# Feed-forward part written out by group, with norms, transposes, beta and gamma beside its matmuls, and x loaded in two pieces

## The chip, the cores and the metric

The kernel runs on one core of a Trainium2 chip, in float32. The metric is the device time of one execution in microseconds (us); of several runs the median counts. The core has five engines with instruction streams of their own: TensorE (PE in the profile, its weight loads PEld), VectorE (DVE), ScalarE (ACT), GpSimd (POOL) and SyncE (SP, which here only issues DMAs). They meet through semaphores alone.

## What is computed

One layer: `xn = norm(x)`, and the output is `x + attention(xn) + ffn(xn)`, where attention normalizes a second time and returns its own residual too.

```python
x = L0_attn_x                                  # (16, 256, 128): 4096 rows of 128
xn = _layernorm(x, axis=-1)
# attention (16 heads of 64, a recurrence over 256 steps), on xn:
xn2 = (xn - mu) / jnp.sqrt(var + LN_EPS) * ln_w + ln_b
beta = jax.nn.sigmoid(xn2 @ Wb.T + bb)         # gamma alike
# ... q, k, v, decays, two states S and R, output projection, + xn
# FFN, on xn:
h = jax.nn.silu(_tlin(x, w1_w, w1_s)) * _tlin(x, w2_w, w2_s)      # 128 -> 512
h = jax.nn.gelu(_tlin(h, h1_w, h1_s), approximate=False)          # 512 -> 512
h = jax.nn.gelu(_tlin(h, h2_w, h2_s), approximate=False)          # 512 -> 512
return _tlin(h, w3_w, w3_s)                                       # 512 -> 128
```

## The kernel before

The 4096 rows lie in 32 tiles of 128 rows, side by side in one SBUF tile `xa` of 128x4096. The program has four stages, one behind the other, and the order in each is written by hand, engine by engine.

**Prologue.** SP issues all loads on one queue: x whole (L239), the constants with the identity (L240), small vectors, then the FFN's weights, all of which count on one semaphore `ld_ffn` (L247 to L254). VectorE and ScalarE normalize all 32 tiles at once, twice: sum and mean (L729, L730), centred rows (L731), squares on ScalarE (L1111), their sum (L735, L736), the root on ScalarE (L1113), reciprocal and product (L738, L739). L741 starts `acc`, to which everything is added. TensorE transposes the 32 tiles of the first norm into the eight PSUM banks and later those of the second norm (L338); ScalarE copies them to `xnT` (L1121) and, with the affine of the second norm, to `xhT` (L1123). TensorE then makes the products of beta and gamma from `xhT` (L345, 128 matmuls with 16 columns), VectorE adds their biases (L746), ScalarE takes the sigmoids (L1129). The weights' wait and that for the biases (`bg_add`) stand ahead of the FFN.

**FFN.** A hardware loop over eight groups of 512 tokens: first layer with its gate (L355, L356, 8 matmuls of 128x512), second (L365, 16), third (L373, 16), last (L379, 16 matmuls with 128 columns). ScalarE does silu (L1136) and gelu (L1139, L1142) between them, VectorE the product with the gate (L754), the last scale and the sum into `acc` (L757, L760). Layers 2, 3 and the last use banks 4 and 5, 6 and 7, and 4.

**Zeroing.** Only behind the last sum (`ffn_added`) VectorE writes ones and zeros into `rst` and the six attention buffers `AS` and `AR` (L764, L766), GpSimd into `lane_id`, `lane_x` and `XF` (L1099). Behind both (`ready`), SP writes the zeros of `XF` to DRAM (L256) and loads the projection weights `wt` (L260); the attention buffers lie where the FFN's were, since the two scopes of SBUF take turns.

**Attention.** 64 quads (4 head groups by 16 batches), software-pipelined by `body(k)` on each engine, written out in full, 32.3 us a quad (2070.2 us by 64). It starts on TensorE with the projections of k and q (L396, L399), which need `wt`.

## Time and profile before

| what | us |
|---|---|
| median of 3 runs (range) | 2472.81 (2470.99 to 2474.99) |
| the profiled execution, its own time | 2473.48 |
| its span | 2471.7 |
| prologue, until the first FFN matmul | 76.6 |
| FFN | 309.3 |
| from there to the first attention matmul | 15.6 |
| attention | 2070.2 |

The span runs from the first to the last instruction that the profile shows; 1.8 us of the execution lie outside it. The four stages are cuts at moments that the trace shows, and add up to the span.

### The profile page before, as it was taken

What the parts mean: (1) busy time and instruction counts of PE and PEld (TensorE: products, weight loads), DVE (VectorE), ACT (ScalarE), POOL (GpSimd) and SP (SyncE); (2) the same over time, 40 slices, a digit from 0 to 9 for tenths busy, and PEclk for the clock granted to TensorE, in tenths of its full rate; (3) what the DMA queues carried; (4) which work ended last, traced back from release to release, by engine and by line L of the source; (5) the groups of instructions that cost most, each with busy time, mean ns of one, the idle gap of its engine ahead of it and who ended that gap; (6) DMA issues with size and microseconds to landing.
All of it is one profiled execution on the core that took longest, in us unless ns stands there. A gap on an engine that the chain in (4) does not pass through costs nothing.

```text
span 2471.7 us, 119622 instructions
## 1 busy us (share of the span) xinstructions
PE 2299.7 (93%) x52544; PEld 1928.8 (78%) x52544; DVE 1754.5 (71%) x3725; ACT 1055.5 (43%) x1616; POOL 1286.6 (52%) x2440
## 2 busy tenths in 40 slices
PE   1999995799999999999999999999999999999997
PEld 1544543588888888888888888888888888888886
DVE  6101013688888878888888788888888888888884
ACT  2323222444444444444444444444444444444430
POOL 0000002656666656666666566666666666666661
PEclk8899997699999999999999999999999999999999
DMA  2000000111111121211111212111112122222221
GB/s 87 1 0 0 0 0 20 27 39 37 37 37 37 37 47 37 39 37 37 37 37 37 43 37 40 37 38 37 37 36 48 38 39 41 41 41 41 41 41 27
DMA packets 306089, 84.77 MB, mean 34 GB/s; under 512 B 280368, under 2 KB 302512, under 8 KB 305584
## 3 DMA queue, kind: packets, MB, share of 16 engines
q1 hardware_dynamic: 305584, 77.25, 15.6%
q8 instruction: 414, 6.78, 1.2%
q14 instruction: 91, 0.75, 0.1%
HBM read 41.53 MB, written 35.65 MB: 31 GB/s over the span
## 4 chain that ended last, share of the span: by engine, by line
PE 59%; issue 20%; DVE 14%; ACT 3%; DMA 2%; SPq 1%; POOL 1%; DVEq 0%; ACTq 0%; POOLq 0%
PE bank L454 10%; PE bank L434 3%; DVE Kt L823 3%; PE bank L416 3%; PE bank L405 3%; PE bank L489 3%; PE bank L498 3%; PE bank L396 3%; PE bank L411 3%; PE bank L613 3%; PE bank L423 2%; PE bank L580 2%; PE bank L399 2%; PE bank L531 2%; PE bank L522 2%
## 5 line engine op out<-in xcount | busy, mean ns | idle before, releaser
L1080 POOL TENSOR_TENSOR lane_t<-lane_n,lane_x 128x15 f32<-128x15 f32 (+7 forms) x960 | 326.7, 340 | 110.2 <-DMA lane_n<-n_dram 34.1
L1083 POOL TENSOR_TENSOR lane_x<-lane_x,lane_t 128x15 f32<-128x15 f32 (+7 forms) x960 | 340.5, 355 | 75.2
L454 PE MATMUL bank<-kq,Kt 64*64 64x96 f32 x8192 | 367.0, 233 | 7.1 <-issue 5.6
L454 PEld LDWEIGHTS bank<-kq,Kt 64*64 64x64 f32 x8192 | 315.2, 134 | 59.3 <-issue 58.9
L1032 POOL TENSOR_TENSOR dk<-cum 128x512 f32<-128x512 f32 x64 | 68.8, 1075 | 297.4 <-DVE cum L800 297.4
L1047 POOL TENSOR_TENSOR KQF<-efull,kn 128x768 f32<-128x768 f32 x64 | 119.5, 1867 | 161.1 <-ACT efull L1196 161.1
L1099 POOL MEMSET lane_id<- 128x256 f32 x1 | 0.3, 312 | 387.1 <-DVE acc L760 387.1
L757 DVE TENSOR_TENSOR dn<-bank,s3b 128x512 f32<-128x512 f32 x8 | 5.5, 692 | 239.5 <-PE bank L379 239.5
L1156 ACT ACTIVATE q<-bank 128x512 f32<-128x512 f32 x64 | 38.2, 597 | 317.3 <-PE bank L399 269.1
L1230 ACT ACTIVATE oS<-bank 128x512 f32<-128x512 f32 x64 | 38.2, 597 | 302.9 <-PE bank L602 302.9
L1165 ACT ACTIVATE ea<-bank,nba 128x256 f32<-128x256 f32 x256 | 107.5, 471 | 124.7 <-PE bank L405 103.3
L800 DVE TENSOR_TENSOR_SCAN cum<-rst,dk 128x512 f32<-128x512 f32 x128 | 157.5, 1231 | 3.3 <-ACT dk L1177 3.3
L777 DVE TENSOR_SCALAR ea<-ea 128x512 f32<-128x512 f32 x64 | 27.7, 433 | 180.3 <-ACT ea L1165 180.3
L851 DVE COPY_PREDICATED AS<-cst,bank 128x384 f32<-128x384 int32 x256 | 142.8, 584 | 16.5 <-PE bank L454 16.2
L823 DVE TENSOR_TENSOR Kt<-ek,kn 128x512 f32<-128x512 f32 x128 | 135.6, 1100 | 0.0
L542 PE MATMUL bank<-AS,yS 64*64 64x64 f32 x2048 | 133.2, 223 | 0.9 <-ACT oS L1230 0.6
L477 PE MATMUL bank<-Zf,dk 64*64 64x32 f32 x4096 | 131.5, 219 | 1.9 <-issue 1.1
L1051 POOL TENSOR_TENSOR KQF<-ea,KQF 128x384 f32<-128x384 f32 x64 | 77.6, 1213 | 103.4 <-ACT ea L1171 103.4
L554 PE MATMUL bank<-yS,AS 64*64 64x64 f32 x2048 | 129.6, 220 | 1.3 <-DVE Sst L883 1.0
L477 PEld LDWEIGHTS bank<-Zf,dk 64*64 64x64 f32 x4096 | 127.3, 136 | 2.6 <-issue 1.6
L598 PE MATMUL bank<-AR,yR 64*64 64x64 f32 x2048 | 128.4, 218 | 0.0
L1048 POOL TENSOR_TENSOR KQF<-efull,q 128x768 f32<-128x768 f32 x64 | 118.5, 1851 | 0.0
(156 smaller groups left out, 6632.4 us busy)
## 6 DMA issues: line engine op xcount, KB each, us to landing
XF<-x_dram SPq DMA_DIRECT2D x256, 64.0 KB, 2.3
lane_n<-n_dram SPq DMA_DIRECT2D x128, 124.0 KB, 2.8
x_dram<-lane_x SPq DMA_DIRECT2D x128, 124.0 KB, 2.3
n_dram<-AS SPq DMA_DIRECT2D x256, 32.0 KB, 2.0
n_dram<-AR SPq DMA_DIRECT2D x256, 32.0 KB, 1.7
wt<-in_win SPq DMA_DIRECT2D x4, 640.0 KB, 4.6
out_y<-acc SPq DMA_DIRECT2D x16, 128.0 KB, 3.0
hw<-in_h1T SPq DMA_DIRECT2D x1, 1024.0 KB, 5.9
```

What stands on the lines that cost most here:

```text
L454: ins = pe.matmul(v3(dst[hd[h], o:o + kinds * C], kinds)[:, :, i * SUB:(i + 1) * SUB], Kt[hd[h], m * 96 + i * SUB:m * 96 + i * SUB + C], r ...
L477: ins = pe.matmul(IV[hd[h], m * SUB:(m + 1) * SUB], P0[hd[h], m * C:(m + 1) * C], v4(Zf[n % 2][hd[h], :], NM, 2)[:, m, :, BASE:], start=Tr ...
L542: pe.matmul(o, pc(yS[c % 2], p)[hd[h], :], prod(n, 0, c, p, 1)[hd[h], :], start=(c == 0 and p == 0), stop=False, skip_group_check=True)
L554: ins = pe.matmul(o, prod(n, 0, c, p, 2)[hd[h], :], pc(yS[c % 2], p)[hd[h], :], start=True, stop=(c == 0), skip_group_check=True)
L598: ins = pe.matmul(o, pc(yR[c % 2], p)[hd[h], :], prod(n, 1, c, p, 1)[hd[h], :], start=False, stop=(c == 0), skip_group_check=True)
L800: dve.tensor_tensor_scan(cum[:, o], rst[:, :], dk[:, o], 0.0, ALU.mult, ALU.add).then_inc(s["cum"], 1)
L823: ins = dve.tensor_tensor(v4(Kt[:, y * 8 * 96:(y + 1) * 8 * 96], 8, 3)[:, :, 0:3:2, :], v4(ek[:, y * 2 * T:(y + 1) * 2 * T], 8, 2), v4(kn[ ...
L851: dve.copy_predicated(v3(dst, reps), mask, v3(src[:, 0:reps * kinds * C], reps)).then_inc(s["pr_sb"], 1)
L1047: pool.tensor_tensor(kv[:, KF_S:KF_R + 1:3], ef, late(kn), ALU.mult).then_inc(s["kf"], 1)
L1048: pool.tensor_tensor(kv[:, QF_S:QF_R + 1:3], ef, late(q), ALU.mult)
L1080: pool.tensor_tensor(tv, lane_n[:, m * SUB + m + 1:m * SUB + BASE].unsqueeze(2).to_broadcast([L, rows, m + 1]), xv[:, m, 0:m + 1].unsqueez ...
L1083: pool.tensor_tensor(xv[:, m + 1:, 0:m + 1], xv[:, m + 1:, 0:m + 1], tv, ALU.subtract).then_inc(s["lane_step"], 1)
```

## The change

The FFN is no longer a loop: its eight groups are written out, with functions `first_layer(g)` to `last_layer(g)`. Between them stand pieces of the former prologue.

- **Loads.** SP issues only the first 4 tiles of x, then `w1` and its scales, then each layer's weights with a semaphore of their own. ScalarE's queue issues the constants, `w2` and the other 28 tiles of x.
- **Norms.** `norm(i, ...)` runs three times on VectorE alone but for the root (the squares are now a VectorE product): tiles 0 to 3 ahead of the FFN; tiles 4 to 31 behind group 0's `hidden`; the second norm, all 32 tiles, behind group 1's. ScalarE's roots for the last two stand between two gelus of the third layer.
- **Transposes** go four at a time through bank 7, in 16 turns: the first ahead of the FFN, then one in group 0, three in each of groups 1 to 4, two in group 5. Beta's and gamma's products follow in two halves, in group 5 ahead of the last layer and in group 6 behind the first; their biases on VectorE are both in group 6, the sigmoids on ScalarE in groups 6 and 7.
- **Banks.** Layers 2 and 3 share banks 4 and 5, the last layer has bank 6.
- **Zeroing** is GpSimd's alone, behind turns 8 and 16. For that `AS`, `AR`, `rst`, `XF`, `lane_x`, `lane_id`, `wt`, `wo` and `ea` have SBUF of their own, at other addresses than before, and SP's zeros and load of `wt` wait only for GpSimd.
- Attention waits for the last sum into `acc`, as before.

TensorE, ahead of the FFN and in its first matmuls: before (`bank<-cst` are transposes, `bank<-wbg` beta's and gamma's products, `w`, `hw` the FFN's weights):

```order
L338 MATMUL bank<-cst,xc 128x128 x32
L338 MATMUL bank<-cst,sq 128x128 x32
L345 MATMUL bank<-wbg,xhT 64x16 x128
L351 UNCONDITIONAL_BRANCH
L351 ISA
L355 MATMUL bank<-xnT,w 128x512
```

and now, from the start to the last layer of group 0:

```order
L349 MATMUL bank<-cst,xc 128x128 x4
L379 MATMUL bank<-xnT,w 128x512
L380 MATMUL bank<-xnT,w 128x512
...
L393 MATMUL bank<-hA,hw 128x512 x16
L406 MATMUL bank<-hB,hw 128x512 x16
L349 MATMUL bank<-cst,xc 128x128 x4
L418 MATMUL bank<-w,hA 128x128 x16
```

and in groups 5 (its end) and 6:

```order
L406 MATMUL bank<-hB,hw 128x512 x16
L367 MATMUL bank<-wbg,xhT 64x16 x64
L418 MATMUL bank<-w,hA 128x128 x16
L379 MATMUL bank<-xnT,w 128x512
...
L380 MATMUL bank<-xnT,w 128x512
L367 MATMUL bank<-wbg,xhT 64x16 x64
L393 MATMUL bank<-hA,hw 128x512 x16
```

Of 320 instructions' worth of transposes and small products, only four transposes still stand ahead of the FFN; the rest stands between its layers.

VectorE in group 0, now (`hA` is the product with the gate, `dn` the scaled last layer; the first row stands behind the norm of the first 4 tiles):

```order
L803 SCALAR_TENSOR_TENSOR hA<-bank,sc,silu 128x512 x4
L787 TENSOR_REDUCE st<-xa 128x28
L788 TENSOR_SCALAR st<-st 128x28
L789 TENSOR_TENSOR xc<-xa,st 128x3584
L790 TENSOR_TENSOR sq<-xc 128x3584
L791 TENSOR_REDUCE st<-sq 128x28
L792 TENSOR_SCALAR st<-st 128x28
L794 RECIPROCAL st<-st 128x28
L795 TENSOR_TENSOR xc<-xc,st 128x3584
L833 TENSOR_TENSOR acc<-xa,xc 128x4096
L815 TENSOR_TENSOR dn<-bank,s3b 128x512
```

Before, the first and the last of these rows followed each other with nothing between; a norm of 28 tiles and the start of `acc` now lie there.

ScalarE in group 0, now (`hB` is layer 2's gelu, `hA` layer 3's):

```order
L1193 DMA xa<-in_x 128x28x128
L1195 ACT_TABLE_LOAD
L1195 ACTIVATE small<-small 128x1
L1199 ACTIVATE st<-st,small 128x4
L1203 ACTIVATE xnT<-bank 128x512
...
L1227 ACTIVATE hB<-bank,sc 128x512 x4
L1227 ACTIVATE hA<-bank,sc 128x512
L1199 ACT_TABLE_LOAD
L1199 ACTIVATE st<-st,small 128x28
L1227 ACT_TABLE_LOAD
L1227 ACTIVATE hA<-bank,sc 128x512 x3
```

The root of the 28 tiles, with a table load on either side, has moved between the first and the second gelu of layer 3. The diff, cut to its core:

```diff
+        AS = ring("AS", 3, NCH * 2 * 3 * C)
+        AR = ring("AR", 3, NCH * 2 * 2 * C)
+        rst = sb("rst", 2 * T)
+        XF = sb("XF", NM * C)
+        lane_x = sb("lane_x", LANE_W)
+        lane_id = sb("lane_id", BASE * BASE)
+        wt = sb("wt", WCOLS)
+        wo = sb("wo", 2 * DM)
+        ea = sb("ea", 4 * T)
...
         @block.sync
         def _(sp):
-            sp.dma_start(xa[:, :].rearrange("p (n m) -> p n m", n=NBLK), x.rearrange("(n p) m -> p n m", p=P)).then_inc(s["ld_x"], 16)
-            sp.dma_start(cst[:, :], consts).then_inc(s["ld_const"], 16)
+            def tiles(t, lo, hi):
+                return t[:, lo * DM:hi * DM].rearrange("p (n m) -> p n m", n=hi - lo), x[lo * P:hi * P, :].rearrange("(n p) m -> p n m", p=P)
+
+            sp.dma_start(*tiles(xa, 0, 4)).then_inc(s["ld_x0"], 16)
+            sp.dma_start(w1[:, :], w1T).then_inc(s["ld_up"], 16)
+            sp.dma_start(sc[:, 0:4], s1).then_inc(s["ld_up"], 16)
+            sp.dma_start(sc[:, 4:8], s2).then_inc(s["ld_up"], 16)
+            sp.dma_start(v3(hw1[:, :], 4), h1T.rearrange("(k p) n -> p k n", p=P)).then_inc(s["ld_h1"], 16)
+            sp.dma_start(sc[:, 8:12], sh1).then_inc(s["ld_h1"], 16)
+            sp.dma_start(v3(hw2[:, :], 4), h2T.rearrange("(k p) n -> p k n", p=P)).then_inc(s["ld_h2"], 16)
+            sp.dma_start(sc[:, 12:16], sh2).then_inc(s["ld_h2"], 16)
+            sp.dma_start(v3(w3[:, :], 4), w3T.rearrange("(k p) n -> p k n", p=P)).then_inc(s["ld_w3"], 16)
+            sp.dma_start(s3b[:, :], s3.partition_broadcast(P)).then_inc(s["ld_w3"], 16)
             sp.dma_start(lnp[:, 0:1], lnw).then_inc(s["ld_small"], 16)
             sp.dma_start(lnp[:, 1:2], lnb).then_inc(s["ld_small"], 16)
             sp.dma_start(wbg[:, :], wbg_in).then_inc(s["ld_small"], 16)
...
-            sp.dma_start(w1[:, :], w1T).then_inc(s["ld_ffn"], 16)
-            sp.dma_start(w2[:, :], w2T).then_inc(s["ld_ffn"], 16)
-            sp.dma_start(v3(hw1[:, :], 4), h1T.rearrange("(k p) n -> p k n", p=P)).then_inc(s["ld_ffn"], 16)
-            sp.dma_start(v3(hw2[:, :], 4), h2T.rearrange("(k p) n -> p k n", p=P)).then_inc(s["ld_ffn"], 16)
-            sp.dma_start(v3(w3[:, :], 4), w3T.rearrange("(k p) n -> p k n", p=P)).then_inc(s["ld_ffn"], 16)
-            for i, w in enumerate((s1, s2, sh1, sh2)):
-                sp.dma_start(sc[:, 4 * i:4 * i + 4], w).then_inc(s["ld_ffn"], 16)
-            sp.dma_start(s3b[:, :], s3.partition_broadcast(P)).then_inc(s["ld_ffn"], 16)
-            sp.wait_ge(s["ready"], 2)
+            sp.wait_ge(s["ready"], 1)
...
-            pe.wait_ge(s["bg_add"], 2)
-            with pe.Fori(0, GROUPS) as gi:
+            def turn(i, src, gr):
+                if i:
+                    pe.wait_ge(s["xnT_sb"], i)
...
+            def first_layer(g):
+                if g == 0:
+                    pe.wait_ge(s["ld_up"], 16 * 4)
+                pe.wait_ge(s["xnT_sb"], g + 1)
                 for o in range(4):
+                    n = 4 * g + o
+                    if n >= 2:
+                        pe.wait_ge(s["h1_sb"], n - 1)
+                    tok = xnT[:, g * FFN_TOK:(g + 1) * FFN_TOK]
...
+            def second_layer(g):
+                if g == 0:
+                    pe.wait_ge(s["ld_h1"], 16 * 2)
+                for o in range(4):
+                    if o < 2 and g:
+                        pe.wait_ge(s["g2_sb"], 4 * g - 2 + o + 1)
...
+            def third_layer(g):
+                if g == 0:
+                    pe.wait_ge(s["ld_h2"], 16 * 2)
                 for o in range(4):
+                    pe.wait_ge(s["g1_sb"], 4 * g + 3 + (o > 0))
...
+            def last_layer(g):
+                if g == 0:
+                    pe.wait_ge(s["ld_w3"], 16 * 2)
+                else:
+                    pe.wait_ge(s["down_used"], g)
                 for tb in range(4):
...
+            turn_xn(0)
+            for g in range(GROUPS):
+                first_layer(g)
+                if 1 <= g <= 2:
+                    turn_xn(3 * g - 1)
+                elif 3 <= g <= 5:
+                    turn_xh(3 * g - 9)
+                elif g == 6:
+                    beta_gamma(1)
+                second_layer(g)
+                if 1 <= g <= 2:
+                    turn_xn(3 * g)
+                elif 3 <= g <= 5:
+                    turn_xh(3 * g - 8)
+                third_layer(g)
+                if g <= 2:
+                    turn_xn(3 * g + 1)
+                elif 3 <= g <= 4:
+                    turn_xh(3 * g - 7)
+                elif g == 5:
+                    beta_gamma(0)
+                last_layer(g)
+
+            pe.wait_ge(s["ffn_added"], GROUPS)
+            pe.wait_ge(s["bg_add"], 2)
...
-                dve.tensor_tensor(n3(cen), n3(src), bc(mean), ALU.subtract).then_inc(s["x_ready"], 1)
-                dve.wait_ge(s["x_ready"], i + 1)
...
+                link(dve.tensor_tensor(n3(tmp), n3(cen), n3(cen), ALU.mult))
                 link(dve.tensor_reduce(var, n3(tmp), axis=AX.X, op=ALU.add))
                 dve.tensor_scalar(var, var, 1.0 / DM, None, ALU.mult).then_inc(s["stat_ready"], 1)
...
-                dve.wait_ge(s["xn_ready"] if i == 0 else s["norm_done"], 1)
-            dve.tensor_tensor(acc[:, :], xa[:, :], xc[:, :], ALU.add).then_inc(s["acc_init"], 1)
...
-                dve.tensor_tensor(v3(bsum[:, n * 512:(n + 1) * 512], 32), v3(bank[n][:, :], 32),
-                                  bbg[:, :].unsqueeze(1).to_broadcast([P, 32, 4 * QD]), ALU.add).then_inc(s["bg_add"], 1)
-            dve.wait_ge(s["acc_init"], 1)
-            dve.wait_ge(s["ld_ffn"], 16 * 10)
-            dve.drain().then_inc(s["ffn_added"], 1)
                 for o in range(4):
-                    dve.wait_ge(s["silu_sb"], gi * 4 + o + 1)
+                    n = 4 * g + o
+                    dve.wait_ge(s["silu_sb"], n + 1)
+                    if g:
+                        dve.wait_ge(s["down_ps"], g)
...
+            norm(0, xa, xc, sq, xc, 0, 4)
+            dve.wait_ge(s["ld_up"], 16 * 4)
+            for g in range(GROUPS):
+                hidden(g)
+                if g == 0:
+                    dve.wait_ge(s["ld_x"], 16)
+                    norm(1, xa, xc, sq, xc, 4, NBLK)
+                    dve.wait_ge(s["xn_ready"], 2)
+                    dve.tensor_tensor(acc[:, :], xa[:, :], xc[:, :], ALU.add).then_inc(s["acc_init"], 1)
+                elif g == 1:
+                    dve.wait_ge(s["acc_init"], 1)
+                    norm(2, xc, sq, xa, sq, 0, NBLK)
+                    dve.wait_ge(s["ld_small"], 16 * 6)
+                    dve.tensor_scalar(nba[:, :], nba[:, :], -1.0, None, ALU.mult).then_inc(s["nba"], 1)
+                elif g == 6:
+                    add_bias(0)
+                    add_bias(1)
+                add_ffn(g)
+
-            dve.memset(rst[:, :], 1.0)
-            for t in AS + AR:
-                dve.memset(t[:, :], 0.0)
-            dve.drain().then_inc(s["zeroed"], 1)
-            dve.wait_ge(s["zeroed"], 2)
-            dve.memset(rst[:, 0:2 * T:C], 0.0)
-            dve.drain().then_inc(s["ready"], 1)
-            dve.wait_ge(s["ready"], 2)
+            dve.wait_ge(s["ready"], 1)
...
-            pool.wait_ge(s["ffn_added"], GROUPS + 1)
-            pool.wait_ge(s["bg_ready"], 1)
+            pool.wait_ge(s["xn_ready"], 3)
+            pool.wait_ge(s["xnT_ps"], 8)
+            for t in AS + AR:
+                pool.memset(t[:, :], 0.0)
+            pool.memset(rst[:, :], 1.0)
+            pool.wait_ge(s["xnT_ps"], 16)
...
-            pool.wait_ge(s["ready"], 2)
+            pool.wait_ge(s["ready"], 1)
+            pool.wait_ge(s["ffn_added"], GROUPS)
+            pool.wait_ge(s["bg_ready"], 1)
...
+            act.dma_start(cst[:, :], consts).then_inc(s["ld_const"], 16)
+            act.dma_start(w2[:, :], w2T).then_inc(s["ld_up"], 16)
+            act.dma_start(xa[:, 4 * DM:].rearrange("p (n m) -> p n m", n=NBLK - 4), x[4 * P:, :].rearrange("(n p) m -> p n m", p=P)).then_inc(s["ld_x"], 16)
+            act.wait_ge(s["consts_set"], 1)
+            act.activation(small[:, 3:4], small[:, 2:3], ACT.Sqrt, bias=small[:, 2:3]).then_inc(s["root_set"], 1)
...
+                    if g < 2 and layer == 1 and o == g:
+                        roots(g + 1, *((4, NBLK) if g == 0 else (0, NBLK)))
+
+            roots(0, 0, 4)
+            keep_xn(0)
+            act.wait_ge(s["ld_up"], 16 * 4)
...
+                if g == 0:
+                    act.wait_ge(s["ld_h1"], 16 * 2)
+                gelus(g, 0)
+                if 1 <= g <= 2:
+                    keep_xn(3 * g)
+                elif 3 <= g <= 5:
+                    keep_xh(3 * g - 8)
+                elif g >= 6:
+                    squash(g - 6)
+                if g == 0:
+                    act.wait_ge(s["ld_h2"], 16 * 2)
+                gelus(g, 1)
...
+            act.wait_ge(s["ffn_added"], GROUPS)
+            act.wait_ge(s["ready"], 1)
             act.wait_ge(s["nba"], 1)
```

## Rows read from the trace of the kernel before

**Rows 1.** Busy time by stage: length, engines' us (instructions), clock, DMA share, GB/s.

```profile
0.00:33.80 33.80, 0.00 (x0) 0.01 (x1) 18.62 (x11) 6.50 (x4) 0.21 (x4) 1.00 0.52 158
33.80:76.60 42.80, 23.05 (x320) 22.49 (x320) 24.12 (x11) 15.80 (x23) 0.00 (x0) 0.68 0.00 1
76.60:385.90 309.30, 308.38 (x896) 150.25 (x896) 33.72 (x46) 87.62 (x117) 0.00 (x0) 0.99 0.00 0
385.90:401.50 15.60, 0.01 (x1) 0.04 (x1) 8.69 (x10) 0.00 (x0) 1.80 (x4) 0.66 0.21 76
401.50:2471.70 2070.20, 1968.31 (x51328) 1756.04 (x51328) 1669.40 (x3648) 945.56 (x1473) 1284.61 (x2432) 0.98 0.19 38
```

**Rows 2.** Timeline of the prologue: start, us, engine, line, out<-in [idle before].

```profile
11.00 4.42 DVE L729 TENSOR_REDUCE st<-xa 128x32 f32<-128x4096 f32 x1 [10.06 <-DMA xa<-in_x]
28.51 0.32 ACT L1113 ACTIVATE st<-st,small 128x32 f32<-128x32 f32 x1 [3.47 <-DVE st L736]
28.87 0.35 DVE L738 RECIPROCAL st<-st 128x32 f32<-128x32 f32 x1 [0.39 <-ACT st L1113]
74.97 1.29 DVE L746 TENSOR_TENSOR bsum<-bank,bbg 128x512 f32<-128x512 f32 x2 [14.03 <-PE bank L345]
75.70 2.02 ACT L1129 ACTIVATE betas<-bsum 128x128 f32<-128x128 f32 x8 [10.86 <-DVE bsum L746]
```

**Rows 3.** DMA issues (us to landing last) and one microsecond's busy time.

```profile
0.80 0.89 SPq L239 DMA_DIRECT2D xa<-in_x  x1
1.75 5.41 SPq L240 DMA_DIRECT2D cst<-in_consts  x1
w<-in_w1T SPq DMA_DIRECT2D x1, 256.0 KB, 2.9
5.00:6.00 1.00, 0.00 (x0) 0.00 (x0) 0.00 (x0) 0.00 (x0) 0.00 (x0) 1.00 1.05 289
```

**Rows 4.** Busy time in single microseconds of transposes and small products.

```profile
58.00:59.00 1.00, 1.00 (x6) 1.00 (x6) 1.00 (x1) 0.93 (x2) 0.00 (x0) 0.50 0.00 0
60.00:61.00 1.00, 1.00 (x12) 1.00 (x11) 0.94 (x2) 1.00 (x3) 0.00 (x0) 1.00 0.00 0
64.00:65.00 1.00, 1.00 (x41) 1.00 (x40) 0.00 (x0) 0.84 (x1) 0.00 (x0) 1.00 0.08 16
67.00:68.00 1.00, 1.00 (x24) 1.00 (x24) 0.00 (x0) 0.00 (x0) 0.00 (x0) 0.50 0.00 0
```

**Rows 5.** Timeline of the FFN's first group and the start of its second.

```profile
76.61 2.07 PE L355 MATMUL bank<-xnT,w 128*128 x2 [1.69 <-DVE bsum L746]
85.52 13.90 PE L365 MATMUL bank<-hA,hw 128*128 128x512 f32 x32
86.44 0.75 DVE L754 SCALAR_TENSOR_TENSOR hA<-bank,sc,silu 128x512 f32<-128x512 f32 x1 [0.99 <-ACT silu L1136]
99.25 13.90 PE L373 MATMUL bank<-hB,hw 128*128 128x512 f32 x32
102.89 0.69 ACT L1142 ACTIVATE hA<-bank,sc 128x512 f32<-128x512 f32 x1 [2.75 <-PE bank L373]
112.98 4.11 PE L379 MATMUL bank<-w,hA 128*128 128x128 f32 x32
```

**Rows 6.** TensorE's waits in the FFN: us in total, times, longest.

```profile
PEld bank L379 <- ACT hA L1142: 2.4, 8, 0.3
```

**Rows 7.** Timeline from the FFN's end to attention's first gate.

```profile
386.75 0.69 DVE L760 TENSOR_TENSOR acc<-acc,dn 128x512 f32 x1
401.49 2.04 PE L396 MATMUL bank<-xhT,wt 128*128 128x256 f32 x4 [15.62 <-DMA wt<-in_win]
405.10 0.60 ACT L1156 ACTIVATE q<-bank 128x512 f32<-128x512 f32 x1 [22.45 <-PE bank L399]
405.71 1.28 ACT L1165 ACT_TABLE_LOAD   x1
407.01 0.84 ACT L1165 ACTIVATE ea<-bank,nba 128x256 f32<-128x256 f32 x2
```

236 lines of the change are left out of this document (118 added, 118 removed).

## The prediction

> **What bounds the kernel now.** I read the busy times by stage first, since shares of the whole span would mix four stages with different limits. The reader is to see there [rows 1] that TensorE has no matmul in the first 33.8 us, is busy 23.05 us of the next 42.8, and that 76.6 us go by before the FFN begins. In the FFN it is busy 308.38 of 309.3 us and nothing else matters. Then it stands still for 15.6 us, and attention takes 2070.2 us with TensorE busy 1968.31 of them. The change does not touch attention's instructions, so the question is how much of 76.6 and 15.6 us goes, and what the FFN has to pay for taking the prologue's work in.
>
> The second view is the timeline of the prologue [rows 2]. It is one chain: x lands at 11.0 us, and each step on 4096 columns takes 4.42 us on VectorE; after two norms come the transposes, then beta and gamma, and the biases at 74.97. The third is the timeline of an FFN group [rows 5], which gives the slots into which the work moves; the fourth is the end of the FFN [rows 7].
>
> **Removed ahead of the FFN.** Its first matmul runs at 76.61 [rows 5]. I work out the new moment, F.
> - The first 4 tiles of x are 256 KB. A load of 256 KB took 2.9 us from issue to landing [rows 3]. It now shares the engines with the constants of the other queue, and at 289 GB/s [rows 3] another 256 KB are 0.9 us. From an issue at 0.8, x is there between 3.7 and 4.6; I take 4.6.
> - The norm of 512 columns: five big steps. By the 4096-column step one would be 4.42/8 = 0.55 us; the 128x512 step that adds the FFN to `acc` took 0.69 [rows 7]. I take 0.65, so 3.25. Two small steps, root (0.32 [rows 2]), reciprocal and handovers: 0.8. Ready at 8.7.
> - Four transposes at half clock: 6 a us [rows 4], 0.65, with the start 0.9. Copy to SBUF 0.60, as the copy of `q` [rows 7], and a handover. F = 10.3.
>
> By then `w1` and `w2`, issued right behind, are there by the same 2.9 us. The gain is 76.61 - 10.3 = 66.3 us, with bounds of 63 and 68 us: F is 8.5 with the lower ends, 13 if the first landing takes 7 us, between these 2.9 and the whole x's 10.1 (11.0 less the issue at 0.8).
>
> The FFN's first layer took 85.52 - 76.61 = 8.9 us for 8 matmuls, where the 16 of the next layer took 13.9 us [rows 5], 7.0 for 8: it began at half clock. That is in the 309.3, and I let it stand, since TensorE is as cold at F as it was at 76.61. The table shows a clock of 1.00 for the first transposes, but no row there has them at 12 a us. The Trainium skill ("TensorE: Matmul & The Clock Gate", What's actually happening) says the throttled clock is the default and activity releases it; that speaks for a cold start too, and no row of this trace shows the start at full rate.
>
> **Removed behind the FFN.** The last matmul ends at 385.9 [rows 1] and attention began at 401.49, when `wt` had landed [rows 7]. Zeros and `wt` are now done during the FFN: GpSimd's memsets and two DMAs, at a time when both have nothing else to do [rows 1]. What is late next is the last sum into `acc`, which ends at 386.75 + 0.69 = 387.44; with a handover attention begins 1.7 us behind the last matmul. Gain 15.6 - 1.7 = 13.9. TensorE also stays warm: the projections of k and q took 3.6 us, 401.49 to the copy at 405.10, at half clock. At full clock they take half, so 1.7 more; from 0 (if the steps behind them catch up) to 3.4 (if the next ones are warm too).
>
> **Added inside the FFN, on TensorE, which has no idle time there.**
> - 15 turns of four transposes. Warm, 12 a us [rows 4], so 0.35 each: 5.2. At half clock 0.65 each, 9.8. I take 5.2, as the FFN runs at 0.99 [rows 1].
> - Six of the inserted pieces stand ahead of a last layer and cover its wait for the last gelu, 2.4 us in eight [rows 6]: 0.3 each, -1.8.
> - Beta and gamma: 128 matmuls in 256 records, 41 a us warm [rows 4], 6.2 us; 24 a us at half clock would be 10.7. I take 6.2.
> - A new wait in group 6: the second half of these products needs bank 7 back, so VectorE's bias for the first half, which stands behind `hidden(6)`. The last `hidden` ends 87.19 - 85.52 = 1.7 us behind the first layer [rows 5], the bias takes 1.29/2 = 0.65 [rows 2]: 2.4 us. On TensorE the second layer is queued behind it.
> - The clock. The small products began at 63.6 at full rate and were at half by 67 [rows 4]. They now come in two runs of 3.1 us, one of them behind the 2.4 us wait. A fall costs what the cold start did, 8.9 - 7.0 = 1.9 us. None is 0, both 3.8; I take one, 1.9, for the run behind the wait.
>
> Sum of the additions: 5.2 - 1.8 + 6.2 + 2.4 + 1.9 = 13.9.
>
> **Work costed at nothing, and its cover.** The norm of 28 tiles on VectorE: `hidden(0)` ends at F + 10.6 = 20.9, four steps of 4.42 x 28/32 = 3.87 and two small ones bring the variances at 36.8. ScalarE reaches the root behind the first gelu of layer 3, at F + 27.0 = 37.3 [rows 5]; table load 1.28, root 0.32, then reciprocal 0.35 and product 3.87 on VectorE: ready at 43.2. TensorE wants it for turn 1 at the end of layer 3, F + 36.4 = 46.7. It has 3.5 us to spare. `acc` starts by 47.6, ahead of the sum into it at 51. The other tiles of x must land by 20.9: until then both queues move 1.05 MB of what is ahead of them and twice 1.84 MB, 4.7 MB at 289 GB/s, which is 16.3 us. The whole x, 2.1 MB, is 7.3 us at that rate and had landed at 10.9, so bytes move from 3.6 at the latest, and the other tiles are there by 19.9. The squares that moved from ScalarE to VectorE are in these steps. The second norm begins at 59.4 (group 1 at F + 40.4 = 50.7, first layer 7.0, last `hidden` 1.7) and has its variances four steps of 4.42 and two small ones later, at 77.5; ScalarE comes for them behind the second gelu of layer 3, at some 79.9. The two extra table loads beside each root delay the next gelu to 40.9 where TensorE needs its bank at 43.2, in group 0; in group 1 they just fit. Four sigmoids (2.02/2 us [rows 2]) with two loads, 3.6 us, begin 0.9 us into layer 3 and end at 4.5; the next gelu must be done by 6.9, two of its four blocks of 3.4 us. The copies are 0.6 us, in stretches where ScalarE waits 2.75 us [rows 5]. Sharing banks 4 and 5 makes the start of layer 3 wait for the third gelu of layer 2, which began one block, 3.4 us, earlier and takes 0.69.
>
> **A rule against this.** A table load shows as 1.28 us, and the next ScalarE instruction starts at 407.01, right behind its end at 406.99 [rows 7]. The Trainium skill ("ScalarE: Activation LUTs", What ACT_TABLE_LOAD costs) counts another 1.38 us of drain for each switch. By the row the loads are covered. By the rule each sigmoid pair would end 2.8 us later and hold TensorE 1.0 us, twice, and those beside the roots some 1.5 together.
>
> **Sum.** Gains 66.3 + 13.9 + 1.7 = 81.9, additions 13.9: 68.0 us. Against the profiled execution, 2473.48 (its span 2471.7 and 1.8 around it, 0.7 above the median), this is 2405.5 us.
>
> **Rivals.**
> - *ScalarE is held by its own DMA queue.* The constants' issue took 5.41 us behind that of the 4096 rows of x [rows 3]. If the issue of the 3584 rows holds ScalarE itself in this manner, shared with SP's queue up to 11 us, the first root comes at some 14.5 instead of 7.5 and F moves by 7: 2412.5. Against it: the issue of x itself took 0.89, only the next DMA was held, and on ScalarE none follows. 8%.
> - *The cover in group 0 fails.* x's rest lands at 30, not at 19.9. Then the 28 tiles are ready at 30 + 15.9 + 0.7 + 3.87 = 50.5, and turn 1 waits 3.8 us: 2409.3. 5%.
> - *Each table switch costs a drain too:* 2405.5 + 3.5 = 2409. The trace shows none. 3%.
> - *The clock falls at many pieces.* 17 pieces in the FFN at 1.9 us each instead of one, +30: 2436. Against it, a turn is 0.35 us of dense work between layers with no gap. 4%.
> - *Slower than before.* Nine attention buffers have new addresses, `AS`, `AR`, `rst`, `ea`, `wt` among them, which are read or written in every quad by several engines. If that cost attention 68.0/64 = 1.06 us a quad of 32.3 (2070.2/64), the gain would be gone; at 1.5 us the time is 2502. No row shows a cost by address. 2%.
> - *It does not do what it says:* TensorE still waits for all of x, or `wt`. The order now shows four transposes ahead of the FFN, so this remains only for the end, 13.9 us: 2419. 2%.
>
> **How the numbers follow.** The forecast has 76%, 2405.5 us. Its own low end is F at 8.5, no fall of the clock and 3.4 us from the warm start: 2405.5 - 1.8 - 1.9 - 1.7 = 2400. Its high end, F at 13, both falls, no gain from warmth, beta and gamma at half clock: + 2.7 + 1.9 + 1.7 + 4.5 = 2416. With the first three rivals inside and the spread of the runs shown (2 us each way) the range is 2399 to 2418. A measurement of this kernel tells 0.2%, 5 us, from no change; every case but the slower one is faster by far more, with 1% for some mixture that comes out even: 97, 1 and 2%.
>
> **What would show each step.** The first 128x512 FFN matmul at 10.3 (8.5 to 13), waiting for ScalarE's copy; root of 28 tiles near 38.6; turn 1 with no wait ahead of it; TensorE idle about 2.4 us in group 6 before its small products, and a half clock behind them; first attention matmul at 335 (401.49 - 66.3 - 13.9 + 13.9), 1.7 us behind the last FFN matmul, at full clock; from there to the end 2070.2 - 1.7. The prediction is wrong if the FFN's own length, without the pieces, moves from 309, if VectorE's chain makes TensorE wait in groups 0 or 1, or if attention's length changes by more than a few us.

## The result and the profile after

The changed kernel took 2415.3 us, median of four runs (2411.7 to 2423.2), beside 2473.9 us for the kernel before in the same session: a ratio of 0.977 with a 95% interval of 0.974 to 0.980, or 58.6 us less. The forecast was 2405.5 with a range of 2399 to 2418: the right side, inside the range, and 10 us too optimistic. A second session, with six runs of the changed kernel, gave 2409.3 against 2470.5 (0.976, interval 0.974 to 0.978), 61.2 us less. The profiled execution took 2418.3 us, with a span of 2416.3.

Busy time by stage, in the columns of [rows 1] (length; busy us and instructions of TensorE, its weight loads, VectorE, ScalarE, GpSimd; clock; DMA share; GB/s):

```profile
0.00:11.59 11.59, 1.11 (x5) 0.74 (x5) 4.09 (x11) 2.63 (x5) 0.21 (x4) 1.00 0.84 257
11.59:341.70 330.11, 326.35 (x1212) 166.31 (x1212) 82.22 (x66) 108.28 (x145) 8.99 (x12) 0.98 0.04 11
341.70:343.30 1.60, 0.04 (x1) 0.04 (x1) 1.38 (x2) 0.00 (x0) 0.00 (x0) 1.00 0.00 0
343.30:2416.30 2073.00, 1966.41 (x51328) 1754.45 (x51328) 1674.47 (x3648) 945.25 (x1473) 1287.90 (x2432) 0.98 0.19 38
```

The prologue has shrunk from 76.6 to 11.6 us and the gap ahead of attention from 15.6 to 1.6. The FFN has grown from 309.3 to 330.1. Attention, whose instructions are the same, took 2073.0 where it took 2070.2.

TensorE's waits up to attention, after (line, what it waited for; us in total, times, longest):

```profile
PE bank L349 <- DVE xc L795: 9.7, 1, 9.7
PE bank L367 <- DVE bsum L809: 2.3, 1, 2.3
PE bank L459 <- DVE acc L819: 1.6, 1, 1.6
PE bank L379 <- DVE hA L803: 1.3, 1, 1.3
PE bank L379 <- ACT xnT L1203: 0.8, 1, 0.8
```

Four of the five were in the forecast. The one for `hA` was not. The timeline of the start shows it (start, us, engine, line, out<-in [idle before]; only the rows that matter here):

```profile
5.10 0.69 DVE L787 TENSOR_REDUCE st<-xa 128x4 f32<-128x512 f32 x1 [4.18 <-DMA xa<-in_x]
9.70 1.11 PE L349 MATMUL bank<-cst,xc 128*128 128x128 f32 x4 [9.70 <-DVE xc L795]
11.59 2.05 PE L379 MATMUL bank<-xnT,w 128*128 128x512 f32 x2 [0.78 <-ACT xnT L1203]
15.32 1.28 ACT L1222 ACT_TABLE_LOAD   x1 [3.87 <-PE bank L380]
16.61 1.27 ACT L1222 ACTIVATE silu<-bank,sc 128x512 f32<-128x512 f32 x2
18.21 1.12 PE L379 MATMUL bank<-xnT,w 128*128 128x512 f32 x2 [1.26 <-DVE hA L803]
23.34 3.88 DVE L787 TENSOR_REDUCE st<-xa 128x28 f32<-128x3584 f32 x1
```

The load of silu's table begins only when the first products are in their bank. TensorE has two pairs of banks ahead of it, then waits for the product with the gate. Before, the same load ran beside the products, since ScalarE came to it behind the sigmoids:

```profile
77.88 1.28 ACT L1136 ACT_TABLE_LOAD   x1 [0.17 <-ACT betas L1129]
```

The last row of the fence before it shows the cover of the long norm holding: it starts right behind `hidden(0)`, and waits for no load. The root of the 28 tiles and turn 1, further on:

```profile
41.18 0.32 ACT L1199 ACTIVATE st<-st,small 128x28 f32<-128x28 f32 x1
41.89 3.89 DVE L795 TENSOR_TENSOR xc<-xc,st 128x3584 f32<-128x3584 f32 x1
49.22 0.60 PE L349 MATMUL bank<-cst,xc 128*128 128x128 f32 x4
```

Ready at 45.8, wanted at 49.2: 3.4 us to spare, where 3.5 were forecast. And group 6, on TensorE and the clock there:

```profile
246.01 3.91 PE L367 MATMUL bank<-wbg,xhT 128*64 128x16 f32 x128
262.93 6.02 PE L367 MATMUL bank<-wbg,xhT 128*64 128x16 f32 x128 [2.25 <-DVE bsum L809]
```

```profile
246.00:250.00 4.00, 4.00 (x130) 3.97 (x130) 0.00 (x0) 1.97 (x2) 0.00 (x0) 1.00 0.00 0
...
262.90:265.00 2.10, 2.08 (x59) 2.10 (x60) 0.00 (x0) 0.00 (x0) 0.00 (x0) 0.80 0.00 0
265.00:269.00 4.00, 4.00 (x75) 3.96 (x73) 0.00 (x0) 0.00 (x0) 0.00 (x0) 0.50 0.02 4
269.00:272.00 3.00, 3.00 (x4) 1.39 (x5) 0.69 (x1) 0.00 (x0) 0.00 (x0) 0.50 0.00 0
```

The first half of beta's and gamma's products ran at full clock in 3.9 us. The second, behind its wait of 2.25 us, ran at full clock for its first 1.3 us, by the granted share of 0.80 of the first 2.1 us, and at half (1.2 GHz) from then on. It took 6.0 us, and the layer behind it took 16.6 us instead of 13.7.

How a row of single microseconds counts has to be read beside this, since two terms of the forecast come from such counts. The first two rows are of the kernel before, in its run of transposes, the third is of the changed kernel, in its first half of small products:

```profile
59.60:60.00 0.40, 0.40 (x5) 0.40 (x4) 0.40 (x1) 0.40 (x1) 0.00 (x0) 0.71 0.00 0
59.60:61.00 1.40, 1.40 (x14) 1.40 (x13) 1.34 (x2) 1.40 (x3) 0.00 (x0) 0.92 0.00 0
247.00:248.00 1.00, 1.00 (x41) 1.00 (x40) 0.00 (x0) 1.00 (x1) 0.00 (x0) 1.00 0.00 0
```

A row counts every record that touches its stretch, also those that began before it and still run. From 60.00 to 61.00 the count grows by 9 (from 5 to 14), so 9 transposes begin in this microsecond, not the 12 of [rows 4]; four of them take 0.44 us. The small products show 41 in one microsecond in the changed kernel too, though its 128 take 3.84 us from the first to what follows them: 33 a us.

### The profile page after: what moved, and what is told of

It reads as the page before. It is cut to its first block, busy times and chain, and to the rows that moved or that the text cites. A ratio compares the mean times of both kernels' runs of the same rounds, so it can differ in the third digit from the quotient of the medians.

```text
span 2416.3 us, 119558 instructions
## 1 busy us (share of the span) xinstructions
PE 2293.9 (95%) x52544; PEld 1921.5 (80%) x52544; DVE 1762.2 (73%) x3727; ACT 1056.2 (44%) x1623; POOL 1297.1 (54%) x2448
## 4 chain that ended last, share of the span: by engine, by line
PE 74%; DVE 12%; issue 8%; ACT 2%; DMA 2%; SPq 1%; POOL 1%; ACTq 0%; DVEq 0%; POOLq 0%
PE bank L517 10%; PE bank L393 5%; PE bank L406 5%; PE bank L497 3%; PE bank L479 3%; DVE Kt L898 3%; PE bank L552 3%; PE bank L468 3%; PE bank L561 3%; PE bank L459 3%; PE bank L474 3%; PE bank L676 3%; PE bank L643 2%; PE bank L486 2%; PE bank L462 2%
## 5 line engine op out<-in xcount | busy, mean ns | idle before, releaser
L393 PE MATMUL bank<-hA,hw 128*128 128x512 f32 x256 | 114.0, 604 | 0.0
```

The costliest lines, as they stand in the source:

```text
L393: ins = pe.matmul(bank[4 + o % 2][:, :], hw1[:, k * HID + o * P:k * HID + (o + 1) * P], hA[:, k * FFN_TOK:(k + 1) * FFN_TOK], start=(k == ...
```

## The experiments

"Start" below is the moment of the first attention matmul: everything up to there is the change's doing, and it is free of what attention itself varies by. After has 343.3 in its first profile, 341.9 in its second, before has 401.5. Apart from the last kernel each experiment was run once. The whole times of such single runs tell little: the kernel before took 2479.9 us in one of their sessions and 2461.3 in the other. So the argument goes by starts and by stretches of the trace.

### The end alone

Theory: of the gain, 14 us come from zeroing and `wt` during the FFN, and the new addresses cost nothing. Rival: they cost attention some tenths of a us in each quad. The kernel before gets the changed one's SBUF layout and GpSimd's zeroing, and nothing else:

```diff
+        AS = ring("AS", 3, NCH * 2 * 3 * C)
+        AR = ring("AR", 3, NCH * 2 * 2 * C)
...
+            pool.wait_ge(s["ffn_added"], 2)
+            for t in AS + AR:
+                pool.memset(t[:, :], 0.0)
+            pool.memset(rst[:, :], 1.0)
...
-            sp.wait_ge(s["ready"], 2)
+            sp.wait_ge(s["ready"], 1)
```

> The kernel before with one part of the change alone: attention's buffers have SBUF of their own at the new addresses, GpSimd alone zeroes them during the FFN, and wt is loaded then. Prologue and FFN loop are as before. Theory: FFN from 76.6 to 385.9, first attention matmul near 387.5 instead of 401.49 (-13.9), the k and q projections at full clock (some 2 instead of 3.6 us), and attention as long as before within the few us that its clock phases cost. Then the head of the program and the pieces inside the FFN account for 387.5 - 343.3 = 44.2 us of the change. Rival (the new addresses cost attention): the start is the same, but attention is over 5 us longer than 2070.2 and its shortest quad is above 30.7 us. Rival (memsets beside the FFN disturb it): the FFN is over 1 us longer than 309.3.

Measured: 2455.6 us. Attention starts at 387.3 instead of 401.5, 14.2 us earlier (13.9 forecast), and takes 2066.5 us, not more than before. Its start:

```profile
387.30 1.13 PE L405 MATMUL bank<-xhT,wt 128*128 128x256 f32 x4 [1.61 <-DVE acc L769]
389.41 0.60 ACT L1166 ACTIVATE q<-bank 128x512 f32<-128x512 f32 x1 [6.95 <-PE bank L408]
```

The gap is 1.6 us and the projections of k and q take 2.1 us at full clock, where they took 3.6 behind the long gap [rows 7]. The addresses cost nothing that can be seen beside attention's own spread (2052.7 to 2073.9 us, below), and not the 68 us that would have undone the gain. By this kernel the rest of the change, the head of the program with the pieces inside the FFN, is worth 387.3 - 343.3 = 44.0 us.

### What makes the clock fall in group 6

Theory A: TensorE's wait does, together with the small products. Theory B: the small products alone do. First the wait is taken away: the bias of the first half moves to group 5.

```diff
-                elif g == 6:
+                elif g == 5:
                     add_bias(0)
+                elif g == 6:
                     add_bias(1)
```

> The changed kernel with VectorE's bias for the first half of beta and gamma in group 5 instead of group 6, so that the second half finds bank 7 free. Theory A (the clock falls because a wait and small products stand together): the wait of 2.3 us goes and with it the fall; the 128 small records take 3.8 us instead of 6.0, the second layer of group 6 13.7 instead of 16.7, and attention starts 7.5 us earlier, at 335.8 instead of 343.3. Rival B (small products alone make it fall, and group 5 was spared by chance): the wait alone goes, attention starts at 341.0, and some clock of 0.50 remains in group 6.

Measured: 2410.8 us, start at 337.4. The wait is gone, the small products follow the first layer with no gap and take 4.0 us. The clock falls all the same, only just behind them:

```profile
260.28 4.02 PE L367 MATMUL bank<-wbg,xhT 128*64 128x16 f32 x128
264.23 11.24 PE L393 MATMUL bank<-hA,hw 128*128 128x512 f32 x22
```

```profile
260.00:264.00 4.00, 4.00 (x127) 3.72 (x128) 0.89 (x2) 1.97 (x2) 0.00 (x0) 0.99 0.02 4
264.00:268.00 4.00, 4.00 (x13) 1.90 (x10) 0.69 (x1) 0.00 (x0) 0.00 (x0) 0.58 0.00 0
```

TensorE's records fill all of these 8 us. The second layer of group 6 took 15.4 us instead of 13.7. The start lies between the 335.8 of A and the 341.0 of B: A is wrong, since no gap is needed, and the fall cost less than B had it. But the wait is not cleared by this. In all six profiles that have it the clock fell within the second half of the small products, 1.2 to 2.7 us after they began. A run of 128 of them with no wait ahead is in nine profiles, eight times in group 5 and here, and the clock fell in three, 3.6 to 3.8 us after the run began. That the wait makes a fall likelier or earlier fits these counts; no run separates it from the place in group 6.

Then both halves in one run in group 5, with a bank for each, so that no wait is left at all:

```diff
-                if half:
-                    pe.wait_ge(s["bg_add"], 1)
...
-                        ins = pe.matmul(bank[7][hd[h], ...
+                        ins = pe.matmul(bank[7 - 7 * half][hd[h], ...
...
                 elif g == 5:
                     beta_gamma(0)
+                    beta_gamma(1)
```

> The changed kernel with both halves of beta's and gamma's products one behind the other in group 5, in banks 7 and 0, and both biases there. No wait, but 256 small records in a row, some 7.7 us. Theory A (a fall needs a wait beside the small products): full clock throughout, attention starts near 335.8 as in the run before. Rival B (a long enough run of small products is enough): clock 0.50 within them or behind them, each such us costing half: 339 to 341.

Measured: 2407.2 us, start at 339.1, where B put it. All 256 records follow each other:

```profile
246.11 8.67 PE L365 MATMUL bank<-wbg,xhT 128*64 128x16 f32 x256
254.71 5.97 PE L418 MATMUL bank<-w,hA 128*128 128x128 f32 x32
```

```profile
246.00:252.00 6.00, 6.00 (x203) 5.89 (x203) 0.69 (x1) 1.97 (x2) 0.00 (x0) 1.00 0.01 3
252.00:256.00 4.00, 4.00 (x68) 3.96 (x65) 0.69 (x1) 0.00 (x0) 0.00 (x0) 0.55 0.01 4
```

Full clock for six us (203 records touch them), then about half (68 in 4 us), with no gap between TensorE's records. The last layer behind them took 5.8 us instead of 3.7. The fall in [rows 4] is in the same small products of the kernel before, there behind a wait of 1.8 us.

### The small products in portions

Theory C: the small products make the clock fall only where many follow each other; 32 records between blocks of the FFN leave it alone. With the bias of the first half in group 5, as above:

```diff
+                    if g == 6:
+                        beta_gamma(1, o)          # 8 matmuls x 2 behind block o of layer 2
...
+                    if g == 5:
+                        beta_gamma(0, o)          # and of layer 3
```

> As e2_bias, but the small products stand in eight portions of 32 records, one behind each block of four FFN matmuls of layer 3 of group 5 and of layer 2 of group 6. The earlier runs showed the clock fall behind small products without any wait too. Theory C (what the clock falls after is a stretch filled by small products; single microseconds of them between dense blocks don't do it): clock 1.00 throughout groups 5 and 6, 0.96 us for each portion, attention starts 1.8 us before e2_bias's 337.4, at 335.6. Rival D (their total within some tens of us counts): the clock still shows 0.50 somewhere in these groups, and attention starts at 337.4 or later.

Measured: 2392.6 us, start at 338.0. One block and its portion, and the clock of both groups:

```profile
232.28 3.60 PE L410 MATMUL bank<-hB,hw 128*128 128x512 f32 x8
235.81 1.11 PE L368 MATMUL bank<-wbg,xhT 128*64 128x16 f32 x32
```

```profile
230.00:250.00 20.00, 20.00 (x143) 10.01 (x142) 0.00 (x0) 3.48 (x6) 1.84 (x5) 1.00 0.18 60
258.00:280.00 22.00, 22.00 (x169) 11.14 (x168) 2.25 (x3) 6.21 (x9) 0.00 (x0) 1.00 0.00 1
```

The clock was 1.00 throughout, as C has it and D does not. With the last kernel, which has portions in group 6 alone, that makes three stretches of portions without a fall. Since a run of 128 without a wait also went without a fall in six of nine profiles, this speaks for C and does not prove it. And the portions are not free. The layer with four of them took 18.59 us, 4.86 more than 13.73, where the whole half in one run took 3.94: 0.23 us for each of the four changes between large and small matmuls. In the second profile of after, small products, wait and half clock together cost 3.9 + 5.2 + 2.3 + 2.1 = 13.5 us; here they cost 9.7, and the 3.8 us between them are those by which attention starts earlier (341.9 to 338.0). Most of this run's gain does not lie there: its attention took 2052.7 us, the shortest of all, for which nothing in the edit gives a reason (below).

### The table load in group 0

Theory: TensorE's new wait in the first layer is silu's table load, begun too late. A tiny activation behind the first copy brings it forward:

```diff
             keep_xn(0)
+            act.activation(small[:, 3:4], small[:, 0:1], ACT.Silu)
```

> The changed kernel with a one-column silu on ScalarE behind the first copy, so that silu's table is loaded at 11.5 and not at 15.3 behind TensorE's first products. Theory: TensorE's wait of 1.3 us in the first layer of group 0 goes, and attention starts 1.3 us earlier, at 342.0. Rival (the first layer is held by the cold clock, not by the table): the wait goes but the layer still takes over 9.8 us of the 10.2, and attention starts at 343.3.

Measured: 2416.1 us, start at 340.4. The load now runs from 11.33 on, beside the first products:

```profile
11.33 1.28 ACT L1234 ACT_TABLE_LOAD   x1
15.31 0.69 ACT L1222 ACTIVATE silu<-bank,sc 128x512 f32<-128x512 f32 x1 [2.48 <-PE bank L380]
```

The first layer took 8.99 us instead of 10.16 and TensorE no longer waited for `hA`: the 8.9 us of the forecast are back. So the load is worth 1.2 us here, and less where the half clock lasts longer and hides it: in after's second profile the wait for `hA` was 0.8 us, with the layer at 10.3 us all the same. Nearly all of the other 1.7 us of the earlier start come from group 6, where the small products took 4.8 us this time: when the clock falls within them is not the same in each execution. The time of the whole kernel does not show the 1.2 us, since attention took 2073.9.

### One queue, and x in one piece

Theory: the first tiles of x land 0.9 us later than alone because the other queue shares the engines with them, as the prediction had it. Rival: the second queue is needed, and without it the first layer waits for its weights. All loads on SP:

```diff
             sp.dma_start(*tiles(xa, 0, 4)).then_inc(s["ld_x0"], 16)
+            sp.dma_start(cst[:, :], consts).then_inc(s["ld_const"], 16)
             sp.dma_start(w1[:, :], w1T).then_inc(s["ld_up"], 16)
+            sp.dma_start(w2[:, :], w2T).then_inc(s["ld_up"], 16)
...
+            sp.dma_start(*tiles(xa, 4, NBLK)).then_inc(s["ld_x"], 16)
```

> The changed kernel with all loads on SP's queue: first tiles of x, constants, w1, w2, the first layer's scales, the other 28 tiles of x, then the other layers' weights. Theory (the second queue buys nothing, since the first wait of VectorE for the rest of x has over 6 us to spare): first FFN matmul within 0.5 us of 11.6, the 28 tiles' norm still begins right behind the last product of group 0 (23.3), attention starts within 1 us of 343.3. Rival: the constants' and w2's later issue moves the first transposes, or layer 2's weights land behind 21.7 and TensorE waits for them: attention starts over 1 us later.

Measured: 2411.0 us, first FFN matmul at 10.22 (11.59 after), start at 340.4. Both are earlier than either theory had them (11.6 and 343.3). Of the 2.9 us at the start 1.4 are the first matmul's; the rest is a shorter half clock in group 6, as in the run before. From issue to landing the same 256 KB, first after, then here (KB each, median us):

```profile
xa<-in_x SPq DMA_DIRECT2D x1, 256.0 KB, 4.3
```

```profile
xa<-in_x SPq DMA_DIRECT2D x1, 256.0 KB, 3.0
```

So the loads on the other queue cost the critical one 1.3 us, more than the 0.9 that the byte rate gives (over the profiles with them it landed 3.9 to 4.4 us after its issue, in the two without 2.9 and 3.0), and the second queue bought nothing: `cst`, `w1` and `w2` were there in time on one. What the single queue changes is SP's time:

```profile
3.84 0.88 SPq L257 DMA_DIRECT2D xa<-in_x  x1
4.76 6.87 SPq L258 DMA_DIRECT2D hw<-in_h1T  x1
```

The issue behind the 3584 rows of x is held for 6.9 us. SP is held so in after too, where those rows are on ScalarE's queue, only at a later load, with nothing urgent behind it:

```profile
5.36 7.41 SPq L260 DMA_DIRECT2D s3b<-in_s  x1
```

So the single queue does not make the hold, it changes which loads stand behind it; what makes it, no run tells. Here layer 2's weights were still in time; see the last kernel for where they are not.

The piece-wise load itself, tested by loading x in one DMA again on SP:

```diff
-            sp.dma_start(*tiles(xa, 0, 4)).then_inc(s["ld_x0"], 16)
+            sp.dma_start(*tiles(xa, 0, NBLK)).then_inc(s["ld_x0"], 16)
```

> The changed kernel with x loaded whole in one DMA on SP's queue; the norm of the first four tiles waits for all of it. Theory: x is there at 10.9 instead of 5.1 and everything up to the first FFN matmul moves by that, 11.6 to 17.4; from there on nothing changes, attention starts 5.8 us later, at 349.1. Rival (the weights now queue behind x and TensorE waits for them in group 0): over 350.

Measured: 2422.2 us, first FFN matmul at 18.2, start at 350.0. x landed at 11.6, against 5.1, and the delay reaches the start of attention: 6.6 us at the first FFN matmul and 6.7 to 8.1 at the start (by the first or the second profile of after; 1.6 us of it is a fall of the clock in group 5 that after did not have, and group 6 lost less than in after's first profile). That is what the two pieces are worth, of the 65.0 us by which the FFN begins earlier; the other 58.4 are what is left for the norm and the transposes of 28 tiles, the second norm, and beta and gamma being no longer ahead, which no run took apart.

### A warm start and a warm end

Theory: the first transposes and the first layer run at half clock because TensorE was idle, and so do the last products; matmuls of no use in both gaps give that back. Rival: they delay what stands behind them.

```diff
+            pe.wait_ge(s["ld_const"], 16)
+            for i in range(3):
+                pe.matmul(bank[0][:, :], cst[:, M_BD:M_BD + P], cst[:, 0:512], start=True, stop=True)
             turn_xn(0)
...
+                    if k == LAST:
+                        keep_warm(k)              # five matmuls of 128x512
                     level0_nx(k)
```

> The changed kernel with eight matmuls of no use: three of 128x512 ahead of the first transposes, once the constants are there, and five while the last quad's inverses travel to DRAM and back, when TensorE otherwise stands still. Theory (the clock after an idle stretch is what varies): the first four transposes take 0.4 instead of 1.1 us, the first layer of group 0 some 8.3 instead of 10.2 us (the table load remains), attention starts 2.5 us earlier, at 340.8; and the drain from the last quad's copy of q to the end is at full clock, near 111 us where before had 112.7 and the changed kernel 117.9. Rival (the drain's length is set by VectorE and the DMAs, not by the clock): it stays at 115 or more, though its clock is 1.00.

Measured: 2403.95 us, start at 339.8.

```profile
4.71 5.49 PE L424 MATMUL bank<-cst 128*128 128x512 f32 x6 [4.71 <-DMA cst<-in_consts]
9.99 0.70 PE L350 MATMUL bank<-cst,xc 128*128 128x128 f32 x4
11.47 1.10 PE L380 MATMUL bank<-xnT,w 128*128 128x512 f32 x2 [0.78 <-ACT xnT L1215]
```

Four transposes in 0.70 us instead of 1.11, the first pair of products in 1.10 instead of 2.05, the first layer in 8.5 us with the table's wait still in it. The clock column reads 1.00 for after's first transposes too, so it doesn't tell there; the durations do. The cold start that the prediction let stand is real, and costs about 2 us; three matmuls are one too many, since they held the transposes until 9.99, 0.3 us longer than in after.

At the end, after's TensorE waits 4.6 us for the last inverses to come back by DMA, and then runs at half clock for 21 us, of which the first window shows the beginning; the second is behind it:

```profile
2376.00:2380.00 4.00, 4.00 (x76) 4.00 (x78) 1.69 (x3) 0.35 (x1) 0.00 (x0) 0.50 0.00 0
...
2400.00:2404.00 4.00, 3.55 (x76) 3.12 (x78) 1.98 (x8) 0.00 (x0) 0.00 (x0) 1.00 0.01 4
```

With the five matmuls the clock was at 1.00 after the gap and the stretch from the last level-0 products to the end took 35.6 us instead of 40.3. The whole drain took 113.8 us, between the 111 of the theory and the 115 of its rival; the clock fell once more further on. But the kernel before, with a gap of 5.7 us in this place, had its clock back within 8 us of it and took 35.3 us. Whether TensorE warms up soon or late here differs between executions of the same instructions: of the ten profiles without the extra matmuls three took 35.1 to 35.3 us (the kernel before, both halves in group 5, the portions), seven 40.3 to 41.3. It is worth 5 us, and both profiles of after were among the seven. So this run alone doesn't show that the five matmuls did it; the last kernel, with 33.0 us and a clock of 1.00 in its last 113 us, speaks for them, though that is one profile too.

### What helped, together

One queue, silu's table load ahead, two matmuls at the start and five at the end, the first bias in group 5, and the second half in portions (the first in one run, which had cost no clock in after):

> All that the earlier runs showed to pay, in the changed kernel: every load on SP's queue (1.4 us), silu's table loaded early and two matmuls of no use ahead of the first transposes (first layer of group 0 in 7.0 instead of 10.2 us), the first half's bias in group 5, the second half's small products in four portions between the blocks of layer 2 of group 6 (no fall of the clock there), and five matmuls of no use in the drain. Sum: first FFN matmul at 10.1, group 0 in 38.5 us, four groups at 39.34, 42.94 and 43.36 us for groups 5 and 6, 40.2 for the last and the start of attention: 332.5, 10.8 us before the changed kernel; the drain 2 to 4 us shorter. Against the changed kernel 11 to 15 us, so 2401 to 2404 where that has 2415. Rival: the dummy matmuls end late and hold the first transposes, or attention's own spread (8 us between profiles so far) hides the gain.

Measured, against the changed kernel in the same session: 2398.6 us, median of six (2392.3 to 2401.6), against 2409.3 (2408.1 to 2413.0), a little less of a gain than expected. The ratio to the kernel before is 0.9705 (0.968 to 0.973) against 0.976. It beats both kernels, by 71.9 and by 10.7 us. Attention starts at 335.5, where 332.5 was expected. Two rows say why:

```profile
18.54 1.98 PE L399 MATMUL bank<-hA,hw 128*128 128x512 f32 x4 [1.51 <-DMA sc<-in_sh]
```

```profile
242.91 3.91 PE L372 MATMUL bank<-wbg,xhT 128*64 128x16 f32 x128
246.75 5.45 PE L426 MATMUL bank<-w,hA 128*128 128x128 f32 x32
```

The second layer now begins early enough to wait 1.5 us for its scales, which stand on SP behind the held issue: the single queue has its price once everything ahead is short. And the first half in one run, harmless in after, here had the clock fall behind it (last layer 5.3 us instead of 3.7), as in one other kernel.

## Why the prediction was right or wrong

The measured numbers are of the profiled execution of after, with its own time 2418.3 where 2405.5 was forecast: 12.8 us. 8.1 of these lie ahead of attention (343.3, forecast 335.2), 4.5 in it (2073.05, forecast 2068.5), 0.2 around the span.

| term | forecast | measured |
|---|---|---|
| first FFN matmul | 10.3 | 11.6 |
| first layer of group 0 | 8.9 | 10.2 |
| 15 turns | 5.2 | 6.6 (0.44 each) |
| cover of the last layer's wait | -1.8 | -2.2 |
| beta and gamma, wait and clock | 10.5 | 15.1 |
| last matmul to attention | 1.7 | 1.6 |
| attention | 2068.5 | 2073.05 |

**The structure was right.** The sum was 9.8 us below the median and inside the range by its upper end; the terms that were off nearly all erred to the same side, so no two errors made the hit. The prologue's chain gone, the whole long norm, both roots with their table loads, the second norm, the squashes and the copies beside the FFN at no cost to TensorE; one new wait in group 6, 2.25 us where 2.4 was worked out; the gap ahead of attention closed, and its projections at full clock. The isolated end gave 14.2 us where 13.9 was summed.

**First FFN matmul, 1.3 us.** Several terms were short. The landing took 4.3 us from the issue and not the 2.9 to 3.8 of the sum, 0.5 us: a load that shares its first microseconds with another queue loses more than its share of the bytes, as the run on one queue showed. A step of 512 columns takes 0.69 us, which the nearest row, of the same shape, had said; 0.65, between that row and an eighth of the long step, was the wrong choice and cost 0.2. The small steps and handovers of the norm took 1.15 us instead of 0.8, the four transposes 1.15 instead of 0.9.

**First layer of group 0, 1.3 us.** The prediction took 8.9 us over as a length of its own. It depended on what ran beside it: silu's table load had been hidden behind work of ScalarE that the change moved away. This is the step that was missed and not merely mis-sized; with the load brought forward the length was 8.99.

**The turns, 1.4 us.** The 12 transposes a us were read off [rows 4], which counts all records that touch the microsecond; 9 begin in it, as shown above. Four take 0.44 us in the kernel before as in a turn of after, so the term was mis-sized by this reading, and a turn between large matmuls costs nothing beside its rate. Portions of small products do: 0.23 us each.

**Beta and gamma, 4.6 us, the largest.** The fall of the clock was foreseen, in the right place, and priced with 1.9 us from the cold start. It cost 2.1 in the small products themselves and 2.8 in the layer behind, and 1.3 and 2.1 in after's second profile. 1.5 us more are the same misreading as in the turns: the 41 a us of [rows 4] are 33, in before as in after, so both halves take 7.7 us and not 6.2. The reason given, the wait ahead of them, is not needed: without the wait the clock fell too, in three profiles of nine, against six of six with it. Whether the wait adds to it stays open. The row that told this was there, in [rows 4], where the small products went to half rate in the midst of TensorE's work; the prediction used its rate and not its meaning. The Trainium skill ("TensorE: Matmul & The Clock Gate", What's actually happening), which tells of half clock as the default, of activity as what releases it and of idleness as what brings it back, would put such a fall down to a gap. Here TensorE's records show no gap (their ends are modelled, so short ones can't be excluded), and the measurement decides.

**The drain behind a table load** did not occur: the load at 15.32 ends at 16.60 and silu starts at 16.61. The rival by the rule of the Trainium skill ("ScalarE: Activation LUTs", What ACT_TABLE_LOAD costs) is out, and so are ScalarE held by its own queue (its issue of 3584 rows took 0.85 us, its first instruction came at 2.85), the late rest of x (landed at 16.8), and the addresses.

**Attention, 4.5 us.** It kept its instructions, and the warm projections gave their 1.5 us. In this profile the excess lies in the drain: from the last level-0 products to the end it took 40.3 us where before had 35.3, while up to there attention took 2032.7 us where before had 2034.9. But its length is not as fixed as the prediction took it: over the ten profiles of kernels without the extra matmuls it went from 2052.7 to 2073.9 us, with 2073.05 in after's first profile and 2065.4 in its second. 5 us of this is the clock in the last 40 us, as shown above. The rest of the spread lies over the quads and is not settled: TensorE's waits for VectorE differ by a few us in total between profiles, and no run was made that tells what moves them. One profile of before could not show this spread, and its 2070.2 was used to a tenth.

## What to carry to other kernels

Take the rate of short instructions from the length of a run of known count, not from the records that one microsecond shows: here that alone was 2.9 us. Ask of each stage left in place what had been hidden beside it. A long run of small matmuls can cost the clock of what follows; in the three stretches tried, portions between large blocks kept it, at 0.2 us each. A second queue for early loads can delay the one that matters, so look at the landing of that one, and at what is queued behind a DMA with thousands of rows.

## What was not expected of the hardware

- TensorE's clock fell from 2.4 to 1.2 GHz with no idle time in the records, in runs of 128x16 products (3.6 us after the run of 128 began in one kernel, 6.3 us after the run of 256 began in another), and in none of three stretches with runs of 32 records between large blocks. In group 5 the same run of 128 left the clock at 1.00 in six profiles and not in two.
- Behind a gap of 4.6 us the clock stayed at half for 21 us of work on 64x64 products with TensorE busy most of the time; in other executions it was back within 8.
- 256 KB landed 3.0 us after their issue with all loads on one queue, 4.3 with the constants and `w2` on another beside them. The issue behind one of 3584 or 4096 rows on the same queue was held for 5.4 to 7.3 us in the kernels that have one; in after, with those rows on ScalarE's queue, a later issue of SP was held for 7.4 us. ScalarE, with no load behind them, was not held.
